# Four graph layers in one program: two generations of source buckets, the last edge rows in columns of 128, split steps in the dense layers too

## What is computed

```
x = x + L0(relu(ln(x)))   # messages by edge type, summed by dst
x = x + L1(relu(ln(x)))   # two neighbour sums:  h = segment_sum(h[src], dst), twice
x = x + L2(relu(ln(x)))   # four GCN layers: x@W, neighbour sum, bias, relu
def L3(x, edge_index, edge_attr, u, ...):
    seg = edge_index[0]                                   # src
    sums = segment_sum(edge_attr, seg)                    # 200000 x 48 into 6250 x 48
    cnt = segment_sum(ones, seg)
    comb = concatenate([x, sums / maximum(cnt, 1), u[batch]])
    return relu(relu(comb @ W1 + b1) @ W2 + b2) @ W3 + b3
x = x + L3(relu(ln(x)))
```

## Time and profile before

| what | us |
|---|---|
| median of 3 runs | 6131.11 (6082.65 to 6141.62) |
| the profiled execution | 6045.54, its span 6043.8 |
| busy in the span: PE, DVE, ACT, POOL | 3482.0, 2609.2, 1504.0, 3119.4 |
| granted share of TensorE's clock | 0.751 |
| first phase, to the start of the sorting beside the neighbour sums | about 3030 |
| six neighbour sums with two dense layers and what lies between | about 2755 |
| last stage | 259 |

### The profile page before, as it was taken

How to read it: one execution, slowest core, us unless ns; L and a number is a source line. 1 busy time by engine, 2 the same in 40 slices (tenths; PEclk the granted TensorE clock), 3 DMA queues, 4 the chain that set the end, 5 groups by cost and what they waited for, 6 DMA issues and landing times.

```text
span 6043.8 us, 84429 instructions
## 1 busy us (share of the span) xinstructions
PE 3482.0 (58%) x18193; PEld 1749.3 (29%) x18194; DVE 2609.2 (43%) x8587; ACT 1504.0 (25%) x3741; POOL 3119.4 (52%) x3191
## 2 busy tenths in 40 slices
PE   4377777777777777776425454345365345364446
PEld 2133333333333333333112121112132112132145
DVE  5266666666666666666250020130120030130188
ACT  2133333333323333332111111111111111111168
POOL 1455555555555555555356655545526645615710
PEclk8588888888888888888667676667667667566679
DMA  5333333333333333333134343234324334324356
GB/s 169 103 82 80 79 78 78 80 79 78 82 78 81 79 78 78 81 78 73 38 102 160 119 157 137 101 113 147 108 79 160 108 126 147 110 78 143 95 206 235
DMA packets 593647, 646.91 MB, mean 107 GB/s; under 512 B 423668, under 2 KB 430418, under 8 KB 587261
## 3 DMA queue, kind: packets, MB, share of 16 engines
q1 hardware_dynamic: 374705, 459.40, 23.2%
q0 software_dynamic: 101760, 110.75, 8.8%
q10 hardware_dynamic: 117068, 75.50, 4.2%
HBM read 451.74 MB, written 190.23 MB: 106 GB/s over the span
## 4 chain that ended last, share of the span: by engine, by line
PE 37%; another core or an unknown queue 22%; issue 20%; DVE 9%; DMA 7%; ACT 2%; DVEq 1%; POOL 1%; SPq 1%; ACTq 0%; POOLq 0%
PE bank L1761 10%; PE bank L1762 7%; PE bank L1766 7%; PE bank L1844 6%; DMA ld_all<-adjacency 3%; DMA rel_table<-ld_all 1%; DVE hid_T L1603 1%; DMA ld_all<-l_sorted 1%; DMA rel_and_z<-adjacency 1%; PE bank L1792 1%; PE bank L1960 1%; PE bank L1894 1%; DVE hid_T L1332 1%; DVE hid_T L1311 1%
## 5 line engine op out<-in xcount | busy, mean ns | idle before, releaser
L713 POOL DMA_INDIRECT l_sorted<-arena,l_pos x1504 | 1487.9, 989 | 1353.7 <-ACT arena L856 896.9
L688 POOL DMA_INDIRECT ld_all<-rel_table,rel_and_z x1564 | 1532.7, 980 | 1114.8 <-remote 474.5
L1761 PE MATMUL bank<-hid_T 128*128 128x400 f16 x2346 | 959.5, 409 | 653.4 <-issue 604.3
L1762 PE MATMUL bank<-hid_T 128*128 128x384 f16 x2346 | 933.0, 398 | 56.3 <-issue 55.9
L1332 DVE TENSOR_SCALAR hid_T<-count_key,hid_T 128x400 f16<-128x400 int16 x2346 | 592.3, 323 | 693.6 <-remote 483.0
L1844 PE MATMUL bank<-rel_and_z,ld_all 128*128 128x512 fp8e4 (+1 forms) x1872 | 509.9, 409 | 538.2 <-issue 487.4
L1844 PE MATMUL bank<-ld_all 128*128 128x512 fp8e4 (+1 forms) x1950 | 521.5, 428 | 371.3 <-DMA ld_all<-adjacency 161.9
L1766 PE MATMUL bank<-ld_all,arena 128*32 x4692 | 519.6, 248 | 119.8 <-issue 119.3
L1761 PEld LDWEIGHTS bank<-hid_T 128*128 x2346 | 254.5, 108 | 1135.4 <-issue 1129.4
L1272 DVE COPY accT<-bank 128x512 f32<-128x512 f32 (+1 forms) x78 | 51.2, 657 | 1224.6 <-remote 707.2
L776 ACT CAST ld_all<-bank 128x400 fp8e4<-128x400 f32 x391 | 191.1, 489 | 1511.5 <-remote 960.1
(11 more groups left out here) (287 smaller groups left out, 4167.9 us busy)
## 6 DMA issues: line engine op xcount, KB each, us to landing
ld_all<-adjacency SPq DMA_DIRECT2D x72, 1600.0 KB
rel_and_z<-adjacency SPq DMA_DIRECT2D x72, 1600.0 KB
l_sorted<-zeros SPq DMA_DIRECT2D x147, 424.0 KB
arena<-in_edge_attr SPq DMA_DIRECT2D x195, 256.0 KB
ld_all<-l_sorted SPq DMA_DIRECT2D x33, 1277.5 KB, 6.0
adjacency<-ld_all ACTq DMA_DIRECT2D x391, 100.0 KB
rel_table<-ld_all SPq DMA_DIRECT2D x49, 520.0 KB, 3.6
ld_all<-rel_table,rel_and_z POOLq DMA_INDIRECT x1564
```

Of the source, the lines that this page charges most:

```text
L688: pool.indirect_dma_start(ring[:, c % RING, 0:TW], None, rel_table, bass.IndirectOffsetOnAxis(ap=rel_i[:, c:c + 1], axis=0)).then_inc(s(f" ...
L713: pool.indirect_dma_start(l3_sorted, bass.IndirectOffsetOnAxis(ap=l3_pos[0:parts, n * SB_K + k:n * SB_K + k + 1], axis=0), rows16[q][0:par ...
L1761: pe.matmul(b0[:, 0:w0], low[:, 0:P], pair_hot[q % 2][:, k, 0:w0], start=k == 0, stop=k == CG - 1)
L1762: pe.matmul(b1[:, 0:GW - w0], low[:, P:2 * P], pair_hot[q % 2][:, k, 0:GW - w0], start=k == 0, stop=k == CG - 1)
```

## The change

Three things.

1. **Two generations of buckets.** Blocks 0 to 41 (FIRST = 42) go to 49 buckets of 30 x 128 rows, blocks 42 to 48 to another 49 buckets of 6 x 128 rows. Places of the second generation start from zero again: after block 41 `l3_held` is set to zero (multiplied by a table that is 0 there) and its value kept in `l3_first`, for the test that no bucket overflows. The bucket's start is put into `l3_pos` ahead of the loop, so `positions` adds two arrays. In the last stage a first loop sums the 49 buckets of generation 0 (30 matrices each, VectorE building 21 columns in 21 instructions, ScalarE nine), while blocks 42 to 46 of m are still split and scattered; a second loop adds generation 1 (six columns, one VectorE instruction), and the MLP moves to this loop. SyncE's wait before the first loop is for m = 0 to 39 alone, and no longer for `late`.
2. **Last rows in columns of 128.** The last 3392 edges lie in 26 columns of 128 rows and one of 64: 27 scatters in place of 32.
3. **Split steps.** AGG_STEPS = 120 of the 135 steps are handed out over the neighbour sums and the dense layers by weights (40 for the first slot of a neighbour sum, 5 for each other one, 9 for a block of a dense layer), the last 15 over the 49 buckets of generation 0. The loops over the dense layers' blocks on ScalarE and VectorE are written out, with a branch on `flag2` in each. In a slot ScalarE's copy now comes ahead of its split step.

Also: the first layernorm's elementwise passes are one instruction in place of 13.

```diff
+GENS = 2
+CAPC = (30, 6)
+CAP = [c * P for c in CAPC]
+FIRST = 42
-DVE_HOTS = 26
+ACT_HOTS = 9
+AGG_STEPS = 120
...
-        def step_piece(step):
-            return step * (2 * NH * 6) // split_steps
-        step_at = {step_piece(step): step for step in range(split_steps)}
+        slots = []
+        for a in range(6):
+            slots += [("agg", 2 * NH * a + i, 40 if i == 0 else 5) for i in range(2 * NH)]
+            if a in (2, 4):
+                slots += [("dense", (a // 2 - 1) * NB + b, 9) for b in range(NB)]
+        span, at, step_at = sum(w for _, _, w in slots), 0, {}
+        for stage, i, weight in slots:
+            step_at[stage, i] = [k for k in range(AGG_STEPS) if at <= (k + 0.5) * span / AGG_STEPS < at + weight]
+            at += weight
+        for t in range(NBK):
+            step_at["bucket", t] = [k for k in range(AGG_STEPS, split_steps) if (k - AGG_STEPS) * NBK // (split_steps - AGG_STEPS) == t]
...
-            sp.wait_ge(s("late"), LATE["sums_wanted"])
             with sp.If(flag2):
                 sp.wait_ge(s("half_mm"), 2 * NH * 6 + 2)
-                for q in range(3):
-                    sp.wait_ge(s(f"l3_moved{q}"), 16 * SB_K * (len(range(q, NSB + 1 - EARLY, 3)) + (q < EARLY)))
...
+                for gen in range(GENS):
+                    whole = (FIRST, NSB)[gen] - EARLY
+                    for q in range(3):
+                        last = gen and (NSB - EARLY) % 3 == q
+                        sp.wait_ge(s(f"l3_moved{q}"), 16 * SB_K * (len(range(q, whole, 3)) + (q < EARLY)) + (16 * REST_DMAS if last else 0))
+                    for t in range(NBK):
+                        n = gen * NBK + t
+                        if n >= 3:
+                            sp.wait_ge(s("node_mm"), n)
...
-                    for k in range(SB_K):
+                    for k in range(SB_K if n < NSB else REST_DMAS):
...
+            def split_step(stage, i):
+
+                for step in step_at[stage, i]:
+                    blk, part = divmod(step, 3)
+                    if part == 0:
+                        split_middle(blk + 2)
+                    elif part == 1:
+                        split_low(blk + 2)
+                    elif blk + 2 < NSB - EARLY:
+                        split_high(blk + 3)
...
-                with act.Fori(0, NB - 1) as b:
+                for b in range(NB - 1):
                     act.wait_ge(s("dense_T"), b + (1 + m0))
                     stage(b + 1)
                     relu(b)
+                    steps(b)
...
-            layernorm(1, G, h).then_inc(s("setup"), 1)
+            layernorm(1, G, h, NT).then_inc(s("setup"), 1)
...
+                    else:
+                        v.tensor_scalar(l3_held[:], held_out, stay[:, bass.ds(n, 1)], None, ALU.mult).then_inc(s("held_ready"), 1)
+                        link(v.scalar_tensor_tensor(l3_first[:], held_out, leave[:, bass.ds(n, 1)], l3_first[:], ALU.mult, ALU.add))
...
+                        v.tensor_copy(node_keys[q][:], keys.rearrange("p k a -> p (k a)")).then_inc(s("node_key"), 1)
+                        v.wait_ge(s("node_key"), n + 1)
+                        for k in range(CAPC[0] - ACT_HOTS):
+                            ins = v.tensor_scalar(node_hot[q][:, k, :], io256[:, 0:P], node_keys[q][:, k:k + 1], None, ALU.is_equal)
+                        ins.then_inc(s("node_hot"), 1)
+                    else:
+                        v.tensor_tensor(node_hot[q][:, 0:CAPC[1], :], io256[:, 0:P].unsqueeze(1).to_broadcast([P, CAPC[1], P]),
+                                        keys.to_broadcast([P, CAPC[1], P]), ALU.is_equal).then_inc(s("node_hot"), 1)
...
                 for t in range(NBK):
-                    node_hots(t, t % 3, t // 3, t % 2)
+                    node_hots(0, t)
                     if t:
-                        node_out(t - 1, (t - 1) % 3)
+                        node_out(0, t - 1)
+                    split_step("bucket", t)
+                for t in range(NBK):
+                    n = NBK + t
+                    node_hots(1, n)
+                    node_out(1 if t else 0, n - 1)
```

More of the change, by code:

```diff
@@ L599, in _ @@
             with sp.Else():
+                sp.wait_ge(s("late"), LATE["sums_wanted"])
                 load_sums(7)
@@ L880, in agg @@
                         m = 2 * NH * a + i
-                        blk, part = divmod(step_at.get(m, -1), 3)
-                        blk += 2
-                        if m in step_at and part == 0:
-                            split_middle(blk)
-                        if m in step_at and part == 1:
-                            split_low(blk)
                         if i % 2:
                             out(m // 2, i // 2 % 2, i // 2 * (HG // TG), min(HG // TG, SRC_T - i // 2 * (HG // TG)))
-                        if m in step_at and part == 2 and blk < NSB - EARLY:
-                            split_high(blk + 1)
+                        split_step("agg", m)
                 with act.Else():
@@ L915, in relu, with steps @@
                     act.activation(xs[:], bank[1][:], ACT.Relu, bias=bias[:]).then_inc(s("dense_relu"), 1)
+                def steps(b):
+                    with act.If(flag2):
+                        split_step("dense", m0 + b)
+                    with act.Else():
+                        act.sem_inc(s("turn"), 1)
                 stage(0)
-                with act.Fori(0, NB - 1) as b:
+                for b in range(NB - 1):
                     act.wait_ge(s("dense_T"), b + (1 + m0))
@@ L1230, in split_less, with split_step @@
                 ins.then_inc(s("split_less"), 1)
+            def split_step(stage, i):
+                for step in step_at[stage, i]:
+                    blk, part = divmod(step, 3)
+                    if part < 2:
+                        split_less(blk + 2, part)
             def power_of_two(t):
@@ L1374, in _ @@
                     link(add_source_term(r, r // 2, r % 2))
-                with fast.over(NG // TG, 2 + 4 + 2 * TG - 1 + 8) as b:
+                with fast.over(NG // TG, 2 + 4 + 2 * TG - 1 + 8 + 1) as b:
                     first = first_of(b * TG)
@@ L1541, in to_u, with steps @@
                                     ALU.mult).then_inc(s("dense_u"), 1)
+                def steps(b):
+                    with v.If(flag2):
+                        split_step("dense", m0 + b)
+                    with v.Else():
+                        v.sem_inc(s("turn"), 1)
                 transposed(0)
-                with ch.over(NB - 1, 1 - n) as b:
+                for b in range(NB - 1):
                     hidden(b)
```

214 lines of the change are left out of this document (124 added, 90 removed).

## The result

The change made the kernel slightly slower: 6196.0 us (6182.4 to 6201.3) against 6131.1 (6082.7 to 6141.6), a ratio of 1.014 with a 95% interval of 1.008 to 1.020. The forecast was 6000. The profiled execution took 6196.0, its span 6194.3. That is 150 more than the profiled execution of before, but 43 of these were there before the first scatter of the split rows (3073 against 3030), and they are no part of the change: in further traces the kernel before made that scatter at 3021, 3024 and 3063 (e8, e11 and e2 have its first phase), the changed one at 3015 to 3074. Another 18 lie between that scatter and the first neighbour sum (75 us in place of 57; 50 to 71 in the other traces), and 2 between the later stages; 87 are left for the stages of the change.

A forecast was written before the change was run, and what follows sets the result against it. GpSimd's bursts of scatters, shutting TensorE off, were taken to make nearly half of the neighbour sums. Neighbour sums -433, dense layers +125, last stage +179, -6 and +5 give -130, from 6131 to 6000 us; range 5860 to 6175.

The forecast's parts named there:

- The stall: Neighbour sums: a burst of 32 scatters is free for some 22 us, then shuts TensorE off for about 22.
- Neighbour sums: Six neighbour sums: 32.3 blocks in place of 43, at 22 us each, 1947 us: -433 (ends -288 and -498).
- the blocks come apart: Neighbour sums: 5.4 blocks in 325 us are 60 us each, against 41 us of scattering; before 55, seven run together.
- The bound of -288: Neighbour sums: the end where a block keeps its old price of 26.5 us, 2092 us in all.
- Last stage: Generation 0 with tail 250, split steps 15, stall 60, generation 1 113: 438 us, +179 (ends +94 and +306).
- the stall among the buckets: Last stage: 155 scatters cost 60 us, half the price of a lone burst; at most 129, at least nothing.
- Dense layers: Two dense layers: 74 + 27 + stalls of about 55 = 156 us each: +125 (ends +52 and +192).
- The rest: First layernorm's passes -6 (0 to -8); first phase's extra VectorE instruction and wait per block +5 (0 to 15).
- The last stage eats it all: Last stage: stall 129, split steps 40, generation 1 at 2.8 per bucket: +306, 6130 us in all; chance 0.20.
- The scatters pile up: Dense layers +192, bursts running on into the next neighbour sum, sums -288: +82, or 6215 us; chance 0.10.
- The lock: Buckets: VectorE's one-hot instructions hold scatters to 3.06 + 0.30 us, generation 1 waits about 200: +70, or 6200; chance 0.05.
- No stall among the buckets: Buckets: one-hot instructions stretch scatters so the stall never sets in, -60; lone blocks at 20, -65: 5875 us; chance 0.13.

The follow-up runs named there:

- e8: The kernel before with a memset of 256 columns after every scatter, so one scatter every 1.59 us; 5771 us, ratio 0.951.
- e11: The kernel before with a memset of 16 columns after every scatter, so one scatter every 1.38 us; 5679 us, ratio 0.939.
- e2: The kernel before with 6 memsets of 848 columns (about 6 to 7 us) after every 16th scatter; 5795 us, ratio 0.952.
- e7: The changed kernel with weight 5 in place of 40 for a neighbour sum's first slot, 7 in place of 9 per dense block; 5962 us, ratio 0.984.
- e3: The changed kernel with a memset of 256 columns after every scatter, so one scatter every 1.59 us; 5651 us, ratio 0.928.
- e14: e7 with all 135 split steps ahead of the buckets, so no scatters in the last stage; 5941 us, ratio 0.979.
- e10: e7 with GpSimd only incrementing a semaphore after every scatter, no memset, still 1.27 us per scatter; 6036 us, ratio 0.993.

## Why the prediction was wrong

The stall was seen rightly, and named as the thing that decides; its price was taken too low at each place, and the three errors have one sign.

1. **Neighbour sums, -433 forecast, -343 measured.** The step that failed: "the blocks come apart: 5.4 blocks in 325 us are 60 us each". They would have, evenly spread; e7's sums took 1882, -495, more than forecast. But the weights put four steps in the first slot of each sum, which was in the code and not worked out: at the start of four of the six sums two or three blocks ran together (bursts of 64, 64, 64 and 96 scatters), and the price stayed at (2034 - 1236) / 31.2 = 25.6 us per block, hardly under the 26.5 of the run-together ones. The bound of -288 was for that.
2. **Last stage, +179 forecast, +260 measured.** The mis-sized term is the stall among the buckets, 60, "half the price of a lone burst, as one-hot building goes on in a stall". It measured 159 (VectorE's nine waits at L1684; the ten buckets' 213 us less ten at the usual pace give 162), over the 129 given as the most. One-hot building does go on, but only for two buckets; and with the small instructions of VectorE and ScalarE beside it the free part ends after 16 us. First to last bucket took 406 us, where 325 was named as the sign. The rest was near: generation 1 took 90 from its first reduce to its last (113 forecast), the one-hot columns 3.52 / 21 = 0.17 each (0.19), the split steps up to 46 (254 in e3 to the 48th bucket, less 208 in e14; 15 forecast, upper end 40). The ends given for this stage, +94 and +306, aren't the sums of its terms, which give +74 and +297; the measured value lies inside either.
3. **Dense layers, +125 forecast, +170 measured**, within its ends (192). The mis-sized term is again the stall: 170 us of "remote" waits at L1596 and L1583, where 55 for each layer, 110 together, was forecast; GpSimd's bursts ran on to 64 there.
4. **The rest.** The first layernorm's passes took 3.62 and 1.89: about -8 (-6 forecast). The first phase's loop: nothing that can be measured (+5 forecast, 0 to 15).

**The rivals.** The outcome lies between the first and the second. *The last stage eats it all* came near in its stage (+260 of its +306), by a dearer stall (159 for 129) and a cheaper generation 1 (90 for 137). *The scatters pile up* was right in its place: behind both dense layers the bursts ran on into the next sum (4361 to 4443, 5242 to 5366), and their first steps took 102 and 131 us. It wanted +82 and the measured change is +65 to +87, but that match is luck: the sums fell further than it said (-343 for -288), and the last stage, which it left as forecast, made up for it. It had a chance of 0.10 because the lump, which made most of it, wasn't seen; with even steps (e7) those two first steps took 55 and 84. *The lock* falls: the 34 scatters that ran beside one-hot instructions alone took 0.97 to 1.04. So what the Trainium skill (SBUF — State Buffer, "SBUF: two separate sides") says of a 2-port mode of VectorE, that it shuts GpSimd out, doesn't show in this case's one-hot rows; whether these instructions run in such a mode, no row tells. The 3.06 of the earlier trace rows was misread: that scatter began beside a TENSOR_TENSOR and only ended beside the TENSOR_SCALAR.

```profile
5771.91 4.45 DVE L1028 TENSOR_TENSOR h<-h,var 128x256 f32<-128x256 f32 x13
...
5776.40 3.50 DVE L1029 TENSOR_SCALAR h<-h 128x256 f32<-128x256 f32 x13
```

All 94 scatters of over 2 us in the 17 traces stand beside a TENSOR_TENSOR that reads f32, which the one-hot instructions aren't; most scatters beside such passes are not that long (median 1.04 in the changed kernel), and what sets the long ones apart stays open.

*No stall among the buckets* falls.

The stall's own nature was taken too literally as time ("free for some 22 us"). It goes rather by how much the engines issue.

## What to carry to other kernels

When an engine that does little in a stage still seems to set its length, look at what runs beside it without a break, as GpSimd's scatters did here, and try a pause there: 0.1 to 0.3 us more after every scatter was worth more (5 to 9%) than any rearrangement of the work (3% at most). Work that is spread by weights should be spread out again by hand before a price per piece is taken: six slots with four steps in each cost 150 us together. And where work is moved off a stage, price it in its new place by what runs there, not by what it cost in the old one.

## What the runs showed of the hardware

GpSimd's indirect DMAs at their closest pace (0.97 + 0.30 us) hold up the other engines once all of them together have issued some 150 to 200 instructions (204 in a neighbour sum after 25 us, 181 among buckets after 16, 155 in the burst below after 46); at 0.06 us more per scatter after 281. In a neighbour sum this doesn't come within a burst of 32 at 1.38 us per scatter, and at 1.47 not at all; among the buckets a little of it is left at 1.47. An instruction in between without added time does nothing (e10). TensorE isn't alone in this. 46 us into the first burst (3073) of the changed kernel, VectorE's passes slow from 0.3 us each to one in 1.4; the order of time:

```profile
3116.91 2.00 DVE L1073 TENSOR_SCALAR h<-h 128x256 f32<-128x256 f32 x8 [0.47 <-DVE h L1072]
...
3119.68 0.70 DVE L1073 TENSOR_SCALAR h<-h 128x256 f32<-128x256 f32 x3 [0.77 <-issue]
...
3121.11 0.29 DVE L1073 TENSOR_SCALAR h<-h 128x256 f32<-128x256 f32 x1 [0.72 <-issue]
...
3122.51 0.29 DVE L1073 TENSOR_SCALAR h<-h 128x256 f32<-128x256 f32 x1 [1.11 <-issue]
```

What it is that piles up stays open. The Trainium skill (NOTIFIC — the notification-queue block, "4.1 Block-level registers (shared by all 10 queues)" and "7.1 Overflow: three behaviours, one of which stalls the engine") tells of a queue that engines' records go through and that can hold back the engine that writes them; no run here shows whether it is this queue. Nor does any show whether the stall is there when nothing is recorded: every execution on record here had its span and granted clock recorded.
